# Reciprocal norms of q applied to the attention scores instead of to q, and the window mask added by the tensor engine

## What is computed

```python
q = l2norm(q) * qs                      # per token and head, over 64 numbers
k = l2norm(k) * ksc
q = q * cos * scale + rotate_half(q) * sin * scale
k = k * cos * inv + rotate_half(k) * sin * inv
# local_attention: a query window of 32 sees its own window and the one before
sim = jnp.einsum('bhwie,bhwje->bhwij', bq, bk2) * QK_SCALE
sim = jnp.where(mask, -jnp.finfo(sim.dtype).max, sim)
attn = jax.nn.softmax(sim, -1)
out = jnp.einsum('bhwij,bhwje->bhwie', attn, bv2)
```

## Time and profile before

| | us |
|---|---|
| median of 3 runs (4414.82 to 4419.62) | 4414.89 |
| the profiled execution | 4412.12 |
| its span, first to last instruction | 4410.3 |
| busy in the span: PE, DVE | 3768.9, 3571.7 |
| busy in the span: POOL, ACT | 2895.4, 2656.4 |

### The profile page before, as it was taken

One profiled execution on the slowest core, in us unless ns is written; L12 is line 12 of the kernel. 1 busy time (PEld: TensorE's weight loads), 2 busy tenths in 40 slices (PEclk: granted clock), 3 DMA queues, 4 the chain that ended last, 5 costly groups with the idle time before them and its releaser, 6 DMA issues. The chain is left out here.

```text
span 4410.3 us, 109941 instructions
## 1 busy us (share of the span) xinstructions
PE 3768.9 (85%) x41516; PEld 2856.2 (65%) x41516; DVE 3571.7 (81%) x5298; ACT 2656.4 (60%) x4035; POOL 2895.4 (66%) x2520
## 2 busy tenths in 40 slices
PE   5666666669999899998999989999899999899996
PEld 3444444357777777776777767777677777677774
DVE  6777777678888788887888878888888888888884
ACT  5666666546666566656566656656566656566663
POOL 3555555357777677676767666777677676667672
PEclk9888888889999999999999999999999999999998
DMA  1111111032222322223222232222322222222221
GB/s 38 53 53 53 53 53 45 8 90 64 55 60 56 92 59 62 56 58 91 62 55 62 56 88 65 55 58 54 89 60 67 56 56 78 70 60 63 56 55 58
DMA packets 157205, 267.21 MB, mean 61 GB/s; under 512 B 32062, under 2 KB 51644, under 8 KB 152380
## 3 DMA queue, kind: packets, MB, share of 16 engines
q1 hardware_dynamic: 157116, 266.19, 22.1%
HBM read 44.81 MB, written 26.21 MB: 16 GB/s over the span
## 5 line engine op out<-in xcount | busy, mean ns | idle before, releaser
L789 POOL TENSOR_TENSOR st_qk_rot<-st_qk_rot,st_qk_sq 128x1024 f32<-128x1024 f32 x384 | 920.4, 2397 | 939.6 <-DVE st_qk_sq L686 939.6
L429 PE MATMUL st_ps<-st_wqkv,st_xs 128*128 128x512 f32 x3456 | 956.7, 412 | 66.2 <-DMA st_wqkv<-wqkv_parts 37.7
L537 ACT ACTIVATE st_qk_sq<-st_ps 128x1024 f32<-128x1024 f32 x384 | 393.9, 1026 | 652.6 <-PE st_ps L429 652.0
L429 PEld LDWEIGHTS st_ps<-st_wqkv,st_xs 128*128 128x128 f32 x3456 | 612.4, 190 | 231.4 <-issue 97.8
L809 POOL TENSOR_TENSOR st_qk_rot<-st_qk_rot,st_rn 128x1024 f32<-128x1024 f32 x384 | 722.7, 1903 | 15.0
L1426 POOL TENSOR_TENSOR at_probs<-at_probs,at_rden 128x128 f32<-128x128 f32 (+3 forms) x512 | 361.8, 738 | 389.6 <-DVE at_rden L1357 389.6
L668 DVE TENSOR_REDUCE st_nt<-st_qk_sq 128x16 f32<-128x1024 f32 x384 | 465.7, 1213 | 175.5 <-ACT st_qk_sq L537 175.4
L686 DVE TENSOR_TENSOR st_qk_sq<-st_ps,st_rot 128x512 f32<-128x512 f32 x768 | 490.2, 678 | 0.0
L672 DVE TENSOR_TENSOR st_qk_rot<-st_ps,st_rot 128x1024 f32<-128x1024 f32 x384 | 465.9, 1213 | 8.6 <-PE st_ps L444 8.6
L444 PE MATMUL st_ps<-consts_sb,st_qk_rot 128*128 128x128 f32 x3072 | 403.0, 274 | 27.9 <-DVE st_hid L769 16.5
L437 PEld LDWEIGHTS st_ps<-st_oT,st_wo 128*128 128x128 f32 x3072 | 368.8, 192 | 79.4 <-issue 75.8
(11 more groups left out here) (125 smaller groups left out, 6828.4 us busy)
## 6 DMA issues: line engine op xcount, KB each, us to landing
st_v_bd<-st_v_tok SPq DMA_DIRECT2D x1152, 128.0 KB, 2.3
st_v_bd<-st_v_tok SPq DMA_DIRECT2D x672, 64.0 KB, 2.1
wqkv_parts<-at_w_parts SPq DMA_DIRECT2D x18, 1024.0 KB, 4.5
st_wqkv<-wqkv_parts SPq DMA_DIRECT2D x18, 1024.0 KB, 5.7
at_w_raw<-in_wqkv SPq DMA_DIRECT2D x18, 512.0 KB, 4.1
rotary_tables<-at_rot SPq DMA_DIRECT2D x6, 512.0 KB, 2.8
st_rot<-rotary_tables SPq DMA_DIRECT2D x24, 128.0 KB, 2.4
st_wo<-in_wo SPq DMA_DIRECT2D x6, 512.0 KB, 4.2
```

What stands on the lines that cost most here:

```text
L429: last = pe.matmul(out[:, c * 512:(c + 1) * 512], xs[:, x_part, t * P:(t + 1) * P], rhs, start=(n == 0), stop=(n == len(PASSES) - 1))
L537: act.activation(qk_sq[:, cols_of(a)], slot_of("qk"[a], 0, t), ACT.Square).then_inc(squared[a], 1)
L789: pool.tensor_tensor(qk_rot[:, cols], qk_rot[:, cols], qk_sq[:, cols], ALU.add).then_inc(rot_done[a], 1)
```

## The change

GpSimd no longer multiplies the reciprocal norms into q (`normalise(0)` is gone), so the transpose of q waits for the rotated q (`rot_done[0]`) instead of the normalised one. The norms go into the scores instead: DVE's pass over the scores multiplies by them where it added the mask before. The mask is added in PSUM by PE: after the 32 small products of a tile, two products of 512 columns with an identity matrix as weights and the mask as moving data, in the float32r format, add the mask to the two banks of scores. The small products now set `start` only for the first in each bank and leave the accumulation open. Identity and mask are rounded to float32r once, by three ACT copies at the beginning of the stack. The mask's value is -1e30 in place of -3e38. Three waits follow: ACT may write new norms only when the scores that use the old ones were taken, DVE waits for the norms before it reads the scores, and the sum of squares waits for the refined norms rather than for the normalised q.

```diff
-    c[:, C_MASK:C_MASK + 2 * WIN] = np.where(first, 0.0, MASKED)
+    c[:, C_MASK:C_MASK + 2 * WIN] = np.where(first, 0.0, MASKED_SCORE)
...
+        ident_r, mask_r = sb("ident_r", [P, P], F32R), sb("mask_r", [P, 2, 2 * WIN], F32R)
...
                 pe.wait_ge(zeroed, 2)
+                pe.wait_ge(rounded, 3)
...
-                                pe.wait_ge(normed[kind == "tk"], tiles_done(u, d, index))
+                                pe.wait_ge(normed[1] if kind == "tk" else rot_done[0], tiles_done(u, d, index))
...
-                                            k_bd[:, c, :, key:key + 2 * WIN], start=True, stop=True)
+                                            k_bd[:, c, :, key:key + 2 * WIN], start=(c % 4 == 0), stop=False)
+                                for c in range(2):
+                                    last = pe.matmul(out[:, c * 512:(c + 1) * 512].rearrange("p (h k) -> p h k", k=2 * WIN),
+                                                     ident_r[:, :],
+                                                     mask_r[:, index > 0, :].unsqueeze(1).to_broadcast([P, HEADS // 2, 2 * WIN]),
+                                                     start=False, stop=True)
...
+                act.activation(ident_r[:, :], ident, ACT.Copy).then_inc(rounded, 1)
+                for i in range(2):
+                    act.activation(mask_r[:, i, :], mask[i], ACT.Copy).then_inc(rounded, 1)
...
                                 act.wait_ge(normed[1], n - 2)
+                                act.wait_ge(taken["sim"], n - 2)
...
-                                dve.wait_ge(normed[a], n - 2)
+                                dve.wait_ge(rn_final, n - 2)
...
+                            dve.wait_ge(rn_final, n - 1)
                             dve.tensor_tensor(scores, slot_of("sim", d1, t1).rearrange("p (h k) -> p h k", h=HEADS),
-                                              mask[0 if t1 == 0 else 1].unsqueeze(1).to_broadcast([P, HEADS, 2 * WIN]),
-                                              ALU.add).then_inc(taken["sim"], 1)
+                                              rn[:, par, heads_of(0)].unsqueeze(2).to_broadcast([P, HEADS, 2 * WIN]),
+                                              ALU.mult).then_inc(taken["sim"], 1)
...
                             reciprocal_norms()
-                            normalise(0)
                             normalise(1)
```

More of the change, by code:

```diff
@@ L43 @@
 MASKED = -3.0e38
+MASKED_SCORE = -1.0e30
 C_IDENT, C_MEAN, C_MASK, C_CAUSAL = 0, P, 2 * P, 2 * P + 4 * WIN
@@ L65, in shape_constants @@
     first = seen & ((np.arange(P)[:, None] >= WIN) | (j >= WIN))
-    c[:, C_MASK:C_MASK + 2 * WIN] = np.where(first, 0.0, MASKED)
-    c[:, C_MASK + 2 * WIN:C_MASK + 4 * WIN] = np.where(seen, 0.0, MASKED)
+    c[:, C_MASK:C_MASK + 2 * WIN] = np.where(first, 0.0, MASKED_SCORE)
+    c[:, C_MASK + 2 * WIN:C_MASK + 4 * WIN] = np.where(seen, 0.0, MASKED_SCORE)
     c[:, C_CAUSAL:C_CAUSAL + P] = np.where(np.arange(P)[None, :] <= np.arange(P)[:, None], 0.0, MASKED)
@@ L241, in local_stack @@
         ff_squared, ff_rstd, ff_xn = sem("ff_squared"), sem("ff_rstd"), sem("ff_xn")
-        gelu_ready = sem("gelu_ready")
+        gelu_ready, rounded = sem("gelu_ready"), sem("rounded")
         ff_gain, ff_newton, pool_own = sem("ff_gain"), sem("ff_newton"), sem("pool_own")
```

## The result

The changed kernel takes 4714.41 us (median of 4 executions, 4710.37 to 4723.09), the kernel before 4414.85 (4 executions, 4405.14 to 4419.62): a ratio of 1.0684, with a 95% interval of 1.0661 to 1.0708. Predicted were 4496 us in a range of 4424 to 4512. The sign was right, and 218 us more were lost than I had reckoned with.

What follows compares the result with a forecast made beforehand. PE's own chain was taken to set the time. Steps costing 0.29, 0.84, 0.29 and 0.45 us, 1.87 a unit times 48, less 8 at the start, gave 82 us more: 4496 us, range 4424 to 4512.

Steps and rivals of the forecast that it cites:

- What bounds the kernel now: Opening part: PE's own chain sets the time, additions count in full unless covering a PE wait; GpSimd reaches PE through DVE.
- The sum: Costs of four steps, 1.87 us a unit times 48, 90 us, less 8 at the start: 82 us slower.
- my rivals: Four alternatives: DVE wins the race 0.25, GpSimd keeps the lock 0.10, mask products cost 0.8 us 0.08, cheap products 0.12.
- my two signs of being wrong: Mask products not spaced for 0.5 us, or DVE's slack in steps 0, 2, 3 used up, so L477 waits longer.
- The pair: PE's two mask products per tile, after the score products: 0.50 us together, 0.25 each.
- The cover by ACT's copy in steps 0 and 2: PE already waits there for ACT's copy L598, so about 0.21 us of the added products is free.
- The relief in step 1: One GpSimd normalisation fewer lets DVE's L656 end earlier, so the output's transpose starts sooner: 0.56 us gained.
- the floor: Earliest start of the probabilities' transpose L449, 8.15 us after the q projection, set by ACT.
- The race: Step 1: GpSimd's normalisation of k starts 0.1 us before DVE's L736 and holds it; step 0.84 us longer; chance 0.45.
- The rival with the race won: DVE's L736 goes before GpSimd's normalisation of k in step 1: 0.56 us a unit, 4434 us; chance 0.25.
- The start: Where the pipeline fills: 8 to 10 us gained over the first two tiles, 8 net, bounds 2 and 12.

Runs made afterwards that it cites:

- e1: Changed kernel with 154 idle semaphore increments ahead of PE's loop, moving it to touch 7 instruction blocks: 4502.31 us, 1.0206 of the kernel before.
- e2: Kernel before with 56 semaphore increments ahead of PE's loop, moving it to touch 8 instruction blocks: 4638.18 us, ratio 1.0514.
- e11: Kernel before with 12 semaphore increments ahead of PE's loop, its end at block 26.89: 4532.48 us, ratio 1.0267.
- e5: Kernel before with 32 semaphore increments ahead of PE's loop, its end at block 26.96: 4648.57 us, ratio 1.0534.
- e7: Changed kernel with 154 increments, and in step 1 GpSimd normalises k only after DVE made the feed-forward input: 4446.18 us, 1.0077 of the kernel before.
- e4: Changed kernel without the mask's two products, scores unmasked, moved by 190 semaphore increments: 4376.33 us, 0.9919 of the kernel before.
- e6: Kernel before with 48 semaphore increments ahead of PE's loop, its end at block 27.03: 4641.49 us, ratio 1.0523.
- e8: Kernel before with two DVE operations issued later: L656 behind q's rotation in step 1, the floor on the sums behind k's products: 4377.71 us, ratio 0.9921.

## Why the prediction was wrong, and where it held

**The step that failed** is the end of "What bounds the kernel now": PE's own chain sets the time, and whatever is added to it counts in full. The sum priced the added products by their time on the array. It left out that they are also instructions in a loop which only just fitted into what PE keeps: four pairs are sixteen compiled instructions of the unit, 28 more stand ahead of it, and its end went from block 26.84 to 27.01. PE then fetched nine blocks in each of 44 repetitions. That the place did it, and not the products, is shown by e1 and e2. The added length of the unit isn't needed for it: 12 and 32 instructions ahead of the unchanged unit brought 21 and 39 reloads (e11, e5). None of my rivals had it, and of my two signs of being wrong it matches neither. The cost to this change is the 212 us between after and e1, which has about 5 of its own for the increments: 217 us, 4.9 for each repetition. Gross it is more. 4.3 us of waiting and some 2 of slow clock are partly given back, because waits behind them shrink: that for the weights from 37.8 us to 17.9, that for the held operation from 47.2 to 21.4 (e1 to after).

The page of before showed 36 instruction packets for a run of 48 units, and its trace none while the loop ran. So it could be read that the loop was kept, and the end of it at 26.84 of 27 could be counted in the compiled program. I did neither. The Trainium skill, Runtime: NRT & Kernel Launch, Instruction fetch mechanics, gives PE a store of 2048 instructions filled in blocks of 256, and says that a branch to code which isn't there waits for a fetch. Eight blocks are 2048 instructions; seven touched and one ahead would fill it. The good kernels have seven and the bad ones load nine at a time, which agrees, but e5 and e11 have seven by my count and reload. The same section of the Trainium skill says that there are only two lines and that no locality is made use of. The trace of before doesn't bear that out for PE: after the first pass, 44 repetitions of 1656 instructions ran without one fetch.

**What held.** Without the reloads the sum is right: e1, moved, takes 4502 us, some 4497 without its increments, against 4496. That it comes within a microsecond is luck: the four steps cost 0.05 less a unit than I had, about 2 us, and the gain at the start was 2 to 4 us smaller. By its terms:

*The pair.* I took 0.50 us, from a spacing of 0.25. The second product starts 0.34 after the first, and the next job 0.57 after the first (2420.39 to 2420.96), so 2.46 us lie between L461 and what follows the pair, not 2.38. The trace of before had this too: the six records of L429 start 0.34 and then 0.23 apart, and I had taken their mean. The next job then takes about 0.1 less, which brings the net cost back to 0.5; e7 less e4 is 0.25, 0.48, 0.25 and 0.42 by steps. In the steps of e1 the change costs 0.27, 0.90, 0.24 and 0.41, where I had 0.29, 0.84, 0.29 and 0.45. The cover by ACT's copy in steps 0 and 2 is there.

*The relief in step 1.* L672 takes 1.08 us for L656's 2.46, and L456 starts 8.15 after q (2368.97 to 2377.12), the floor that I had counted. Without the mask, step 1 gains 0.86 (e4); the prediction's 0.56 and L494's own wait of 0.31 make 0.87.

*The race.* L826 of k was put at 14.05 after q and the bias at 14.15; they came at 14.15 and 14.20. The order held, in all 39 units, by half the margin that I had given it. The sum itself was slightly off there: 12.8 + 1.29 is 14.09, not 14.05, which leaves a margin of 0.06, and 0.05 was measured. A race that close, against an error of mine as large, was called right with some luck. L753 ends 0.29 after L826 (0.33 predicted), L506 starts at 16.65 (16.59). e7 shows that the race is the cause: without it step 1 is 1.28 shorter. In the changed kernel itself it is lost only in 21 of 39 units, those in which L823 started first; the reloads are what differs from e1, where it is lost in all.

*The rival with the race won* was 0.56 a unit; e7, which forces it, has 0.54 (71.48 - 70.94).

*The start* was put at 8 to 10 us gained. From the first projection to the transpose of the second step's q it was 47.15 us before (897.01 to 944.16) and is 41.35 after (894.10 to 935.45): 5.8, and 3.7 in e1. The wait for L809 went from 7.71 to 0.91, but the transpose of k behind it waits 3.91. This term was too large, and within the bounds that I gave.

*Readings.* "No other engine is near that" was too strong, since DVE is busy for 81% where PE has 85%. Other slips are of 0.01 or 0.02 us in a term, and the last sum, 4412.1 + 82 + 2.8, gives 4497. None of them changes the forecast.

**What stays open.** Why e2, e5, e6 and e11 escape some reloads, and where exactly the edge lies, was not settled. A stream that starts some tens of instructions ahead of my count, together with a fetch that is sometimes decided in time, would give this order, but no run shows it. The traces have a hint. All the escapes of e2, e5 and e6 (2, 5 and 2 of 44) are at the five layer borders, and there a single instruction packet came 3.0 to 3.4 us before the next unit's first projection. At the borders with a reload, in after, e2 and e6, the first packet came earlier, 7.8 to 8.7 us before it. In e11 the heads that escape have no packet or a single one 3.0 to 5.8 us before the projection. So whether the block ahead is fetched before the branch may decide; no run tests it. That the store holds eight blocks is argued from the figure of the Trainium skill and the packets; no run measured it by itself.

## What to carry to other kernels

A loop on TensorE has a size and a place. Here the place decided: 1672 instructions were kept at one place (e1), and 1656 were loaded again and again at another (e2). If the profile shows instruction packets that grow with the number of repetitions, and a wait for "issue" at the loop's head, count the blocks of 256 instructions that the loop touches, and leave room: an end at 26.84 was kept, one at 26.89 not always. Moving the loop was worth 212 us here, the best reordering of the work 36. Measure a small edit to such a loop at two places before its time is put down to the edit. And where DVE and GpSimd meet in SBUF, who comes first by a few hundredths of a microsecond decides about a whole instruction: put the short DVE operations where they meet no GpSimd operation or one with little left to run, as e8 does for 36 us.

## What the runs showed of the hardware that I had not expected

A unit of 1656 or 1672 instructions on TensorE was either kept (36 or 37 packets in all) or loaded whole, nine packets of 16.4 KB, in a repetition. One reload makes PE wait 4.3 us at the branch, six products of 512 columns then take 2.92 us for 1.66 at a granted clock of 0.59, and the net price was 4.9 to 6.0 us (after and e5). Twelve increments of a semaphore ahead of the loop cost 2.7%, 32 cost 5.3%, and 190 cost 0.2%. Near the edge the outcome isn't one or the other for a kernel but for each repetition: 21, 39, 42 or 44 of 44 were loaded again.

A DVE operation between operands in SBUF that came 0.04 to 0.09 us after a GpSimd one took 2.09 to 2.15 us instead of 0.48, in all 39 units of e1.
